# A selective scan block: eight of 32 state inputs made by ScalarE and TensorE instead of GpSimd, five more output products moved to GpSimd, and new places for the next row's front

## What is computed

```python
xn = layernorm(x)
def scan_block(x, x_proj_w, dt_proj_w, dt_proj_b, A_log, Dp):
    A = -exp(A_log)
    delta, B, C = split(x @ x_proj_w.T, [32, 48])
    delta = softplus(delta @ dt_proj_w.T + dt_proj_b)
    # for each channel and state: h[t] = exp(delta*A) * h[t-1] + delta*x*B[t]
    y = sum over states of h * C
    return y + Dp * x
s = scan_block(xn, ...) + reversed(scan_block(reversed(xn), ...))
sel = argmax of a small router on the last token
f = gelu(xn @ W1[sel] + b1[sel]) @ W2[sel] + b2[sel]
g = silu(xn + 0.3 * (f @ Wo + bo))
out = x + s * g
```

## Time and profile before

| | |
|---|---|
| median of 3 runs | 3575.49 us (3574.2 to 3582.67) |
| the profiled execution | 3578.16 us, its span 3576.3 us |
| first scan starts | 102.92 us |
| busy shares | VectorE 95%, GpSimd 92%, TensorE 67%, ScalarE 63% |
| mean granted clock of TensorE | 0.84 |

### The profile page before, as it was taken

How to read it: one execution, slowest core, us unless ns; L and a number is a source line. 1 busy time by engine, 2 the same in 40 slices (tenths; PEclk the granted TensorE clock), 3 DMA queues, 4 the chain that set the end, 5 groups by cost and what they waited for, 6 DMA issues and landing times. The chain is left out here.

```text
span 3576.3 us, 44870 instructions
## 1 busy us (share of the span) xinstructions
PE 2409.3 (67%) x12086; PEld 1836.7 (51%) x12086; DVE 3389.1 (95%) x2315; ACT 2262.5 (63%) x3452; POOL 3301.1 (92%) x1550
## 2 busy tenths in 40 slices
PE   6667676666666666666667666666676666666665
PEld 4455554555555555455555545554455545555554
DVE  2899999999999999999999999999999999999999
ACT  3666666656666666666666666566666666666663
POOL 1899999999999999999999999999999999999997
PEclk8888888888888888888888888888888888888886
DMA  5333243433333433333332433333333333333332
GB/s 157 114 125 118 96 134 125 131 116 117 105 123 129 131 109 110 120 123 125 130 112 95 134 125 131 114 117 107 122 130 130 108 108 123 125 125 125 112 104 75
DMA packets 217920, 425.59 MB, mean 119 GB/s; under 512 B 38860, under 2 KB 113365, under 8 KB 217813
## 3 DMA queue, kind: packets, MB, share of 16 engines
q1 hardware_dynamic: 217812, 424.56, 36.4%
HBM read 382.54 MB, written 25.18 MB: 114 GB/s over the span
## 5 line engine op out<-in xcount | busy, mean ns | idle before, releaser
L437 POOL TENSOR_TENSOR bx<-dx,b_sb 128x1024 f32<-128x1024 f32 x1024 | 2396.9, 2373 | 49.5 <-DVE hs L738 48.0
L738 DVE TENSOR_TENSOR_SCAN hs<-decay,bx 128x1024 f32<-128x1024 f32 x1024 | 2318.8, 2277 | 105.9 <-POOL bx L437 48.3
L651 ACT ACTIVATE decay<-delta,rate 128x512 f32<-128x512 f32 (+1 forms) x2048 | 1326.7, 681 | 902.3 <-DVE hs L738 893.9
L932 PE MATMUL y<-ident,hc 128*128 128x128 f32 x8192 | 1240.6, 306 | 49.0 <-DVE hc L723 48.3
L932 PEld LDWEIGHTS y<-ident,hc 128*128 128x128 f32 x8192 | 1109.9, 160 | 297.0 <-issue 154.1
L915 PE MATMUL c<-dbc,selector 128*128 128x512 f32 x864 | 489.8, 567 | 1072.9 <-DVE hc L723 1071.9
L723 DVE TENSOR_TENSOR hc<-hs,c 128x1024 f32<-128x1024 f32 x864 | 1031.8, 1194 | 22.0 <-PE c L915 21.8
L915 PEld LDWEIGHTS c<-dbc,selector 128*128 128x128 f32 x864 | 186.9, 216 | 1263.5 <-DVE hc L723 1253.1
L423 POOL TENSOR_TENSOR hc<-hs,c_sb 128x1024 f32<-128x1024 f32 x160 | 378.2, 2364 | 2.6 <-DVE hs L738 2.3
L411 POOL TENSOR_TENSOR lg<-lg,ex 128x1024 f32<-128x1024 f32 x64 | 151.1, 2361 | 175.7 <-ACT lg L554 174.4
L892 PE MATMUL front<-w2o_sb,hT 128*128 128x256 f32 x1024 | 299.8, 421 | 4.1 <-ACT hT L564 4.1
(11 more groups left out here) (117 smaller groups left out, 1510.9 us busy)
## 6 DMA issues: line engine op xcount, KB each, us to landing
b_sb<-b_scratch SPq DMA_DIRECT2D x512, 512.0 KB, 3.7
c_sb<-b_scratch SPq DMA_DIRECT2D x160, 256.0 KB, 4.0
xin<-in_L_attn_x_dram SPq DMA_DIRECT2D x32, 512.0 KB, 5.0
w_sb<-in_L_ffn_W_dram SPq DMA_DIRECT2D x32, 512.0 KB
w2o_sb<-w2o_scratch SPq DMA_DIRECT2D x32, 512.0 KB
xres<-in_L_attn_x_dram SPq DMA_DIRECT2D x32, 512.0 KB, 6.4
out_dram<-og SPq DMA_DIRECT2D x32, 512.0 KB, 5.5
dbc<-high SPq DMA_DIRECT2D x64, 128.0 KB, 2.3
```

The lines of the kernel that those rows point to most:

```text
L437: nc.gpsimd.tensor_tensor(bx[:, s % RING, :, :], dx[:, par, g, :, :], b_sb[:, s // GROUP % GRING, s % GROUP, :].unsqueeze(1).broadcast_to( ...
L651: A(dps[s % DSLOTS][:, k, cols], delta[:, par, g, k, cols], ACT.Exp, scale=rate[:, g, k, n:n + 1]).then_inc(s_decay, 1)
L738: V.tensor_tensor_scan(hs[:, s % HSLOTS, :, :].rearrange("p k t -> p (k t)")[:, u], dps[s % DSLOTS][:, :, :].rearrange("p k t -> p (k t)") ...
L932: ins = M(yps[:, c, k * P:(k + 1) * P], hc[:, s % RING, k, c * P:(c + 1) * P], ident[:, :], start=False, stop=(s == ADDED[-1]), is_transpo ...
```

## The change

For the eight states in TURNED, dx * B isn't made by GpSimd. TensorE turns dx once a row and direction into token layout (`turn_dx`), ScalarE copies it to SBUF (`copy_dxT`); B too is turned (`turn_b`, `copy_btok`), so that B of a state is one number per partition. ScalarE then scales four pieces of 128 x 256 (`scale_dx`), and TensorE turns them back (`turn_bx`), right into the PSUM slot that holds the decay of other states. The decay of these eight states goes to an SBUF buffer of two places, `decay_sb`. B is loaded for one state at a time, in a ring of eight.

GpSimd makes ten products with C instead of five, and their additions lag by three steps instead of two. Nearly all places of the front are new. `delta` and `dx` have fewer copies; weights used only at the start share space with the new buffers.

```diff
-    MEAN, SCALE, SHIFT, NORM = 0, 1, 5, 6
-    TRANS, XNT, PROJECT, HIGH, LOW = (7, 8), (8, 9), (9, 10), 11, 12
-    EXPAND, ABS = (14, 15, 16, 17), (15, 16, 17, 18)
-    EXP, LN, SQUARE, RATIO = (17, 30), (18, 31), (19, 32), (20, 33)
-    FFN_IN, HIDDEN, GELU = (18, 19, 20, 21, 22, 23, 24, 25), (20, 22, 24, 26), 27
-    POOL_C, C_LAG, ADD_LAG = (3, 9, 15, 21, 27), 3, 2
+    TSLOTS = 2
+    MEAN, SCALE, SHIFT, NORM = 0, 1, 4, 6
+    TRANS, XNT, PROJECT, HIGH, LOW = (6, 7), (8, 9), (8, 9), 11, 12
+    B_TURN, B_COPY = 11, 13
+    EXPAND, ABS = (14, 15, 21, 22), (16, 17, 23, 24)
+    EXP, LN, SQUARE, RATIO = (18, 25), (19, 26), (20, 27), (21, 28)
+    DX_TURN, DX_COPY = (27, 28, 44, 45), (29, 30, 46, 47)
+    FFN_IN, HIDDEN, GELU = (16, 16, 17, 17, 18, 18, 19, 19), (19, 20, 21, 22), 30
+    TURNED, SCALED_AT, TURN_LEAD = (6, 9, 12, 15, 22, 25, 28, 31), (2, 5, 8, 12, 18, 22, 25, 28), 3
+    POOL_B = [s for s in range(STEPS) if s not in TURNED]
+    POOL_C, C_LAG, ADD_LAG = (3, 6, 9, 12, 14, 17, 19, 22, 25, 28), 3, 3
...
+            def scale_dx(row, par, i):
...
+                wait(act, s_bxT, row * NT + i - TSLOTS + 1)
+                for c in range(C):
+                    A(dxb[:, i % TSLOTS, c, :], dxT[:, g, c, :], ACT.Copy, scale=btok[:, par, c, g, n:n + 1]).then_inc(s_dxb, 1)
...
                 for k in range(DT):
                     cols = slice(0, T) if k != later else slice(1, T) if g == 0 else slice(0, T - 1)
-                    A(dps[s % DSLOTS][:, k, cols], delta[:, par, g, k, cols], ACT.Exp, scale=rate[:, g, k, n:n + 1]).then_inc(s_decay, 1)
+                    A(to[:, k, cols], delta[:, g * (1 + par), k, cols], ACT.Exp, scale=rate[:, g, k, n:n + 1]).then_inc(s_decay, 1)
...
+                    if s in SCALED_AT:
+                        scale_dx(row, par, SCALED_AT.index(s))
...
+                if s in TURNED:
+                    i = TURNED.index(s)
+                    dve.wait_ge(s_bxT, row * NT + i + 1)
+                    data, factor = dps[s % DSLOTS][:, :, :], decay_sb[:, i % TSLOTS, :, :]
...
+            def turn_dx(row, i, last):
...
+                for c in range(2):
+                    for k in range(DT):
+                        at = c * D + k * P
+                        ins = nc.tensor.transpose(fps[:, at:at + P], dx[:, g, k, (2 * half + c) * P:(2 * half + c + 1) * P], ident[:, :])
...
             def ffn_in(row, par, j, k):
                 if k == 0:
-                    unit(row, 7 + j)
-                    pe.wait_ge(s_w, row * 64 + 64)
+                    if j == 0:
+                        pe.wait_ge(s_relu, row * 4 + 2)
+                        pe.wait_ge(s_w, row * 64 + 64)
+                    else:
+                        pe.wait_ge(s_hid, row * FT + j)
...
+            def turn_bx(row, i):
+
+                s = TURNED[i]
+                pe.wait_ge(s_dxb, row * C * NT + C * i + C)
+                wait(pe, s_scan, row * STEPS + s - DSLOTS + 1)
+                for k in range(DT):
+                    for c in range(C):
+                        ins = nc.tensor.transpose(dps[s % DSLOTS][:, k, c * P:(c + 1) * P],
+                                                  dxb[:, i % TSLOTS, c, k * P:(k + 1) * P], ident[:, :])
+                ins.then_inc(s_bxT, 1)
...
+                    if s + TURN_LEAD in TURNED:
+                        turn_bx(row, TURNED.index(s + TURN_LEAD))
```

More of the change, by code:

```diff
@@ L357, in _ @@
             move_bc(0, 0)
-            for j in range(GRING - 1):
+            for j in range(BRING - 1):
                 load_b(0, 0, j)
@@ L377, in body @@
                             load_expert(row + 1)
-                    if i * GROUP == 12 and not last:
+                    if POOL_B[i] == 11 and not last:
                         if not second_last:
@@ L404, in step_x @@
                 pool.wait_ge(s_xnT, row * 2 + 2)
[L406 to L407 removed]
+                wait(pool, s_dxturn, (row - 1) * 2 * DT + g * DT + DT)
+                nc.gpsimd.tensor_tensor(dx[:, g, :, :], delta[:, g * (1 + par), :, :], xnT[:, par, :, :], ALU.mult).then_inc(s_dx, 1)
             def log1p(row, g):
@@ L533, in absolute @@
                 A(ex[:, g, k, :], bank[:, :], ACT.Abs, bias=dtb[:, g, k:k + 1]).then_inc(s_abs, 1)
-                wait(act, s_dx, (row - 1) * 2)
-                wait(act, s_decay, (row - 1) * 2 * STEPS)
-                A(delta[:, par, g, k, :], bank[:, :], ACT.Relu, bias=dtb[:, g, k:k + 1]).then_inc(s_relu, 1)
+                wait(act, s_dx, (row - 1) * 2 + 1 - g)
+                wait(act, s_decay, (row - 1) * DT * STEPS + (1 - g) * DT * N)
+                A(delta[:, g * (1 + par), k, :], bank[:, :], ACT.Relu, bias=dtb[:, g, k:k + 1]).then_inc(s_relu, 1)
             def exp_abs(row, g):
@@ L580, in front @@
                     high_part(row)
+                if s == B_COPY:
+                    copy_btok(row, par)
+                if s in DX_COPY:
+                    copy_dxT(row, DX_COPY.index(s))
                 if s in ABS:
@@ L868, in expand_delta @@
             def expand_delta(row, par, q):
                 g, k = q // DT, q % DT
-                bank = unit(row, 3 + q)
+                if q == 0:
+                    pe.wait_ge(s_btok, row + 1)
+                    wait(pe, s_dxT, row * 4)
+                elif q == 2:
+                    pe.wait_ge(s_hid, row * FT + FT)
+                else:
+                    pe.wait_ge(s_relu, row * 4 + q)
                 if q == 0:
                     pe.wait_ge(s_dbc, row * 64 + 64)
-                M(bank[:, :], dtw_high[:, g, k, :], dbc[:, par, g, :], start=True, stop=False)
@@ L888, in ffn_out @@
                 if part % 4 == 0:
-                    unit(row, 11 + v)
-                    pe.wait_ge(s_gelu, row + 1)
+                    if v == 0:
+                        pe.wait_ge(s_dxT, row * 4 + 2)
+                        pe.wait_ge(s_gelu, row + 1)
+                    else:
+                        pe.wait_ge(s_zz, row * 2 + 1)
                 for j in range(half * 2, half * 2 + 2):
@@ L896, in ffn_out, with front @@
                         ins.then_inc(s_pf, 1)
-            def front(row, par, s):
+            def front(row, par, s, last=False):
                 if s in TRANS:
@@ L1013, in body @@
                         broadcast_c(row + 1, 1 - par, 0)
+                    if s + TURN_LEAD in TURNED:
+                        turn_bx(row, TURNED.index(s + TURN_LEAD))
                     if s == 0:
                         skip_term(row, par)
-                    front(row, par, s + STEPS)
+                    front(row, par, s + STEPS, last)
                     if not last:
```

206 lines of the change are left out of this document (122 added, 84 removed).

## The result

| | before | after |
|---|---|---|
| median | 3576.60 us (3574.2 to 3582.67, 4 runs) | 4466.16 us (4460.1 to 4475.51, 4 runs) |
| ratio, 95% interval | | 1.2486 [1.2459, 1.2513] |
| span of the profiled execution | 3576.3 us | 4473.7 us |
| TensorE's mean granted clock | 0.84 | 0.81 |

The change makes the kernel 25% slower. The forecast had the sign and most of the mechanism, but its 4006 us is 460 us short, and its range (3800 to 4150) does not hold the result.

A forecast was written before the change was run, and what follows sets the result against it. VectorE was taken to bound the kernel at 108.4 us a row; after the change 99.8 of work plus waits of 9.7, 5.8 and 7.0 make 122.3 us a row, 4006 us in all, with a range of 3800 to 4150.

The forecast's parts named there:

- This would be a gain of 31 x 5.55 = 172 us: Five more products with C leave VectorE, 5.55 us a row: the gain if nothing else happened.
- Places A and B: VectorE's products 18 and 21 wait for additions behind the second and fourth hidden tiles' matmuls on TensorE: 9.7 and 5.8 us a row.
- the ring: VectorE's products have four buffer places, so product 18 must wait until TensorE's addition of state 14 is done.
- The smaller ones: Products 16, 10, 29, 31 and four more wait for late pooled additions: 6.0 us a row at full clock, 7.0 taken.
- T(16): The moment at which VectorE is through with scan 16.
- the last row has no front and gets the gain, -6: The last row carries no next row's front, so it was to be 6 us faster, without the waits.
- up to 17 at the low one: Upper bound of the smaller waits' sum, us a row, with TensorE at its low clock.
- a little over half of this distance: Range's upper end: 127 us a row, 4150 us in all, between full clock (117.3) and low clock everywhere (134.6).
- GpSimd hides nothing of this: GpSimd is in nobody's way: its products are ready before the waits end, SyncE's loads seven states of B ahead.
- The waits are covered: Rival: VectorE binds as now without the new waits, 102.8 us a row, 3401 us; chance 8%.
- no change: Rival: product 18 isn't held, only broadcast 20 comes late, 108.4 us a row, 3578 us; chance 3%.
- TensorE at full clock: Rival: slower, but TensorE stays at 2.4 GHz throughout because of its added work, 3851 us; chance 15%.

The follow-up runs named there:

- e12: Kernel after with front spaced, C rows loaded earlier, pooled additions first in TensorE's step, one scaling a step later, lag 2: 3458.40 us, ratio 0.9661.
- e1: Kernel after with the additions of states moved ahead of the front's matmuls in each step of TensorE's queue: 3984.73 us, ratio 1.1145.
- e2: Kernel after with one number undone, the lag of pooled additions 2 steps instead of 3: 3893.82 us, ratio 1.0879.
- e11: Kernel after, lag still 3, with a pooled state's addition first in its step on TensorE: 3885.91 us, ratio 1.0856.
- e4: Kernel after with the front spaced out: expansions in steps 14 to 17, hidden tiles at half a tile a step in 18 to 25: 4039.76 us, ratio 1.1299.
- e6: Kernel after, nothing moved, with transposes adding zeros (40 in step 17, 28 in step 19) to keep TensorE busy: 4361.82 us, ratio 1.2187.
- e8: Kernel before with one number of the change, the lag of pooled additions 3 steps instead of 2: 3823.61 us, ratio 1.0689.
- e3: Kernel after with SyncE's loads of C rows asked for three products with B earlier: 4361.69 us, ratio 1.2199.
- e5: Kernel after with three edits together: additions ahead of the front, front spaced out, C rows loaded earlier: 3558.68 us, ratio 0.9948.

## Why the forecast was right or wrong

**What binds.** Right: VectorE bound before, and a row was its work plus 3.0 us. "This would be a gain of 31 x 5.55 = 172 us" was right in kind as a potential: e12, all of the change's work in another order, has seven tenths of it, 122 us below the kernel before (3458.40 against 3580.05 us, measured side by side).

**VectorE's work**, 99.8 us a row: measured 100.6. Products of 1208 ns where 1194 were read make 0.3 of the difference. The rest is probably strokes broken by waits: in e12, which has few, the work is 100.0.

**Places A and B**, 9.7 and 5.8: measured 9.6 and 5.8. Terms, chain and clock as written: in the mean of 30 rows the four matmuls take 3.8 us at place A and 3.7 at B, at a granted clock of 0.51, and the addition at A 1.3 (1.45 taken). e1, e2 and e11 show the ring (the wait before product 18 goes with the place of one addition), e4 the hidden tiles.

**"The smaller ones ... so I take 7.0"**: measured 14.8 a row. This is the step that failed, 7.8 x 31 = 242 us of the missing 460 (14.5 x 31 = 450 of these are in the 31 rows). The places and the form were right, the lengths were not: they were summed at nearly the full clock, since "the mean granted clock of 0.85 means three tenths of the time at the low level". In the 6 us before each product, the mean granted clock of the 30 rows and the wait were:

| product | granted clock | wait, us | forecast at full clock |
|---|---|---|---|
| 10 | 0.83 | 2.4 (1.45 in the rows above 0.85) | 1.5 |
| 29 | 0.94 | 2.1 | 2.0 |
| 23 | 1.00 | 0.4 | 0.2 at most |
| 16 | 0.51 | 3.9 | 1.6 |
| 7, 13, 26 | 0.61, 0.67, 0.60 | 1.8, 1.7, 1.7 | 0.2 at most each (up to 1.5 at the low one) |

Where the clock was full, the forecast's terms come out; where it was low, they fall short by 1.5 to 2.3 us each. Product 16, in the row shown for places A and B (T(16) is 2226.94):

```profile
2229.51 0.80 PE L942 MATMUL front<-dbc,dtw_high 128*128 128x512 f32 x1 [0.61 <-ACT delta L568]
...
2230.53 3.36 PE L1023 MATMUL y<-ident,hc 128*128 128x128 f32 x16
...
2233.93 1.22 DVE L767 TENSOR_TENSOR hc<-hs,c 128x1024 f32<-128x1024 f32 x1 [3.68 <-PE y L1023]
```

Delta's Relu is through at T(16) + 2.5 (2.6 forecast). Then the expansion takes 1.02 us for 0.47 and the two additions 3.36 for 1.84, at a granted clock of 0.55, and the product starts at T(16) + 7.0 where 4.9 was summed. No run gives these places a full clock and leaves the rest alone; e6 raised it in parts and took 0.4 to 0.9 us off four of them. The low clock isn't all of it, either: e8 shows a wait of 1.07 us in such a window with TensorE at full clock. Even the last row of the kernel after, which carries no next front, waits at these places (products 13, 16 and 21):

```profile
4401.98 1.22 DVE L767 TENSOR_TENSOR hc<-hs,c 128x1024 f32<-128x1024 f32 x1 [1.88 <-PE y L1023]
...
4413.09 1.22 DVE L767 TENSOR_TENSOR hc<-hs,c 128x1024 f32<-128x1024 f32 x1 [2.20 <-PE y L1023]
...
4429.13 1.22 DVE L767 TENSOR_TENSOR hc<-hs,c 128x1024 f32<-128x1024 f32 x1 [1.63 <-PE y L1023]
```

so "the last row has no front and gets the gain, -6" was wrong as well: from output product to output product it takes 110.6 us (4466.25 - 4355.62), some 9 more than the 101.6 in the kernel before.

The 0.85 was read from the kernel before, and used for a kernel in which VectorE has twelve times the idle time (36.2 us a row for 3.0). In such waits TensorE has idle times of its own (7.43 and 4.07 us at places A and B), and it comes back at the low level, where an addition takes some 1.9 us for 1.04. The sum's own upper bound, "up to 17 at the low one", was nearer than its value. That the upper end of the range took "a little over half of this distance" had the same fault.

**"GpSimd hides nothing of this ... SyncE's loads are ahead by seven states of B"**: true of B, and nothing was said of C, whose loads stand in the same queue behind the wait for `low`. 3.7 us a row, 115 us; e3 gives 104. The order of the queue showed it, had both kinds of load been followed through it.

**Not foreseen:** 1.4 us a row at the loop's start, 43 us, and 0.9 of waits before the output product and between. The kernel before has 0.9 us a row before the same scan, put down to GpSimd's bx, which the forecast expected to go; so 0.5 is new. In the kernel after it is "issue"; the instruction queues carry 153 and 185 packets in this kernel, 19 and 89 in the one before. No run took it away in the kernel after, so its cause stays open. Together: 100.6 + 9.6 + 5.8 + 14.8 + 3.7 + 1.4 + 0.9 = 136.8 us a row, against 122.3.

**Rivals.** "The waits are covered" (3401 us) and "no change" were rightly held small; place A decided as said. TensorE at full clock (3851 us) was wrong in its direction: the clock fell.

**What the profile should show.** Two gaps of 9.05 and 5.42 us in the row shown, released by additions; GpSimd at 69% (under 80%); scans of 2276 ns with the decay in PSUM and 2279 with bx there instead: all as written. Matmuls follow hT at once, after 4.07 us of idle at place B, but 7.43 at A (4 to 6 said). VectorE's products are idle for 30.2 us a row, not some 20, and its share is 72%, not 82: this is the missing 14.5 us a row.

**Decay into SBUF.** It takes 708 ns an operation there and 677 in PSUM by the groups of line 693, 0.03 us more. The Trainium skill (ScalarE: Activation LUTs, Step-by-step: what each stage is for) says that ScalarE writes PSUM faster than SBUF, and this trace agrees in direction. It is under the 0.1 us allowed, and no scan waits for a decay in SBUF in the kernel after.

## What to carry to other kernels

When an order is loosened by one step, list for every ring what stands between "its slot is freed" and "its slot is needed", and sum that at the low clock too. The distance in steps alone says little: in the kernel before, lag 3 cost 7% or nothing by the place in the step.

Work that frees a buffer goes first in its step, before work that only has a later use; and a queue with a wait in it is followed for every kind of transfer behind the wait.

When the engine that bound the kernel starts to wait, the clock of TensorE, for which it waits, can fall too (here from 0.84 to 0.81). Sum the small waits of the changed kernel with the durations of the low level, not with the old kernel's mean.

## What was unexpected of the hardware

- Waits and the clock go together: at the same 14614 matmuls TensorE's granted clock was 0.81, 0.86, 0.89 and 0.93 in kernels of 4466, 3894, 3491 and 3458 us, and its busy time 2909, 2706, 2570 and 2483 us. It isn't in step with the time everywhere: e5, at 3559 us, had 0.91. That the low clock lengthens the waits in its turn is shown by e6 alone, at place B and at four of the small ones.
- Zero additions helped as far as they reached up to the work they were for: behind 1.0 us of idle time four matmuls took 1.98 us, behind 2.4 us 2.62, and the addition after them 1.91.
- The releaser that the profile names in brackets was in one place a bystander that ended at the same time (TensorE's addition before GpSimd's product 12). The sum over the group named the load of C, and e3, which moved this load, took the wait away.
